# A fused cross-attention and ternary feed-forward kernel: loads issued earlier, and value products of two key chunks issued in pairs

## What is computed

```python
q = rope((layernorm(x) @ Wq)); k, v = split(ctx @ Wkv); k = rope(k)
w = softmax(q k^T / 4)
x = x + (w v) @ Wout + bout
u = layernorm(x)
h = gelu(bitlinear(u, w_fc))
out = x + bitlinear(h, w_proj)
# bitlinear(x, w): layer norm, x_hat = clip(x*128/max|x|) * max|x|/128,
#                  w_hat = sign(round(w/(mean|w|+eps))) * mean|w|
```

## Time and profile before

| | before |
|---|---|
| median of 3 runs | 849.15 us |
| the profiled execution | 848.58 us, span 846.5 us |
| projection, first scores | 0 to about 142 us |
| first turned scores | 172.8 us |
| last weighing of values | 556 us |
| rows | to 846.5 us |
| PE busy | 784.4 us (93%) |
| DVE busy | 681.3 us (80%) |
| ACT busy | 454.3 us (54%) |
| POOL busy | 337.8 us (40%) |

### The profile page before, as it was taken

The page is one execution under the profiler, slowest core; times in us unless marked ns, Lnnn a source line. Parts: engine busy times, 40 slices in busy tenths (PEclk is TensorE's granted clock), DMA queues, the critical chain, the costliest instruction groups (busy, mean ns, idle before and its releaser), DMA issues.

```text
span 846.5 us, 11693 instructions
## 1 busy us (share of the span) xinstructions
PE 784.4 (93%) x3842; PEld 334.0 (39%) x3842; DVE 681.3 (80%) x937; ACT 454.3 (54%) x825; POOL 337.8 (40%) x428
## 2 busy tenths in 40 slices
PE   1999997499999999999999989887999999999995
PEld 0788885023223223222232222233444444444442
DVE  5888885588888888888888868157999899988883
ACT  4466664067777777777777757642322432233230
POOL 3688875364445544555444535312222111111000
PEclk9999998589999999999999989999999999999999
DMA  8288877634455555676655773224466535654463
GB/s 273 83 216 233 253 189 168 163 90 118 120 154 149 143 155 135 148 144 163 163 143 142 201 134 85 71 74 79 110 117 137 120 87 108 112 117 88 83 128 88
DMA packets 175579, 116.14 MB, mean 137 GB/s; under 512 B 116512, under 2 KB 147232, under 8 KB 175520
## 3 DMA queue, kind: packets, MB, share of 16 engines
q1 hardware_dynamic: 175520, 115.40, 56.1%
HBM read 64.50 MB, written 25.43 MB: 106 GB/s over the span
## 4 chain that ended last, share of the span: by engine, by line
PE 80%; DVE 7%; DMA 5%; SPq 3%; ACT 2%; issue 2%; POOL 1%; DVEq 0%; POOLq 0%; ACTq 0%
PE banks L638 15%; PE banks L625 14%; PE banks L599 12%; PE banks L879 11%; PE banks L867 10%; PE banks L256 9%; PE banks L853 5%; DMA stack_words<-max_rows 2%; PE banks L280 1%; SPq L230 1%; DVE h_scales L945 1%; SPq L526 1%; ACT probs_words L689 1%; PE banks L246 1%; DVE probs_words L954 1%
## 5 line engine op out<-in xcount | busy, mean ns | idle before, releaser
L669 DVE TENSOR_REDUCE maxima<-banks 128x2 f32<-128x1024 f32 x256 | 302.1, 1216 | 67.2 <-PE banks L599 67.1
L689 ACT ACTIVATE probs_words<-banks 128x512 f32<-128x512 f32 x512 | 276.3, 597 | 105.3 <-PE banks L625 103.5
L625 PE MATMUL banks<-stack_words 98*128 98x512 bf16 x512 | 175.7, 386 | 6.6 <-DMA stack_words<-max_rows 4.6
L599 PE MATMUL banks<-stack_words 96*128 96x512 bf16 x512 | 160.8, 397 | 9.1 <-DMA stack_words<-k_parts 4.8
L638 PE MATMUL banks<-probs_words,late_words 128*32 128x512 f32 x1024 | 137.2, 608 | 0.5
L867 PE MATMUL banks<-ternary_words,late_words 128*128 128x512 f16 x512 | 114.6, 382 | 8.1 <-DMA late_words<-late_words 8.1
L879 PE MATMUL banks<-ternary_words,stack_words 128*128 128x512 f16 x512 | 114.6, 383 | 5.4 <-DMA stack_words<-stack_words 5.4
L995 ACT ACTIVATE probs_words<-probs_words,h_moments 128x2048 f32<-128x2048 f32 x16 | 32.0, 2002 | 130.9 <-DVE h_moments L937 130.9
L625 PEld LDWEIGHTS banks<-stack_words 98*128 98x128 bf16 x512 | 39.4, 97 | 147.9 <-ACT probs_words L689 85.4
L599 PEld LDWEIGHTS banks<-stack_words 96*128 96x128 bf16 x512 | 50.0, 100 | 73.9 <-DVE maxima L669 12.3
L879 PEld LDWEIGHTS banks<-ternary_words,stack_words 128*128 128x128 f16 x512 | 50.3, 99 | 71.4 <-issue 15.3
(11 more groups left out here) (123 smaller groups left out, 935.0 us busy)
## 6 DMA issues: line engine op xcount, KB each, us to landing
o_rows<-late_words SPq DMA_DIRECT2D x32, 256.0 KB, 2.7
k_parts<-ternary_words SPq DMA_DIRECT2D x48, 128.0 KB, 2.5
q_parts<-ternary_words SPq DMA_DIRECT2D x48, 128.0 KB, 2.4
stack_words<-q_parts SPq DMA_DIRECT2D x32, 192.0 KB, 2.9
stack_words<-k_parts SPq DMA_DIRECT2D x96, 64.0 KB, 2.7
stack_words<-k_parts SPq DMA_DIRECT2D x32, 192.0 KB, 2.8
attn_words<-in_x_dram SPq DMA_DIRECT2D x16, 256.0 KB, 4.1
probs_words<-in_L_ffn_w_fc_dram SPq DMA_DIRECT2D x16, 256.0 KB, 3.6
```

The lines of the kernel that those rows point to most:

```text
L599: mm = self.nc.tensor.matmul(self.score_slot[j % 2][:, i], self.mem.q_stack[0:STACK, slot, head, c * P:(c + 1) * P], self.mem.k_stack[0:ST ...
L625: self.nc.tensor.matmul(self.mem.banks[:, self.ST_BANK[k]], self.mem.k_stack[0:STACK + 2, slot, head, c * P:(c + 1) * P], self.mem.q_stack ...
L669: dve.tensor_reduce(self.maxima[:, g % 2, 2 * j:2 * j + 2], self.score_slot[j % 2], AX.X, ALU.max).then_inc(self.scores_read, 1)
L689: act.activation(self.probs[:, c, head, :], self.mem.banks[:, self.ST_BANK[k]], ACT.Exp, scale=1 / math.sqrt(HEAD)).then_inc(self.exp_done, 1)
```

## The change

In `tensor_step` the four chunks of values are no longer weighed one at a time at c = 0, 1, 2, 3 but two at once at c = 0 and two at c = 2. On SP the weights of the first two blocks and two of the first four stacks are loaded before the projection's end, the loads of Wout, its bias and the first rows of x are spread over eight steps. On POOL the first `split_maxima` stands ahead of the first `ternarise`, and two divisions later. On DVE `save_sums` follows the second reduction of a step instead of the first, and the last inversion stands one step later. On ACT the first `centre_u` stands among the exponentials.

```diff
--- before.py
+++ after.py
@@ -649,9 +649,11 @@
             if 0 <= turned < GROUPS:
                 self.scores_turned(pe, turned, 4 * c + 1)
             if c == 0 and before >= 0:
-                self.weigh_v(pe, before, CHUNKS - 1)
-            if c > 0 and 0 <= turned < GROUPS:
-                self.weigh_v(pe, turned, c - 1)
+                self.weigh_v(pe, before, 2)
+                self.weigh_v(pe, before, 3)
+            if c == 2 and 0 <= turned < GROUPS:
+                self.weigh_v(pe, turned, 0)
+                self.weigh_v(pe, turned, 1)
             if 0 <= turned < GROUPS:
                 self.scores_turned(pe, turned, 4 * c + 2)
                 self.scores_turned(pe, turned, 4 * c + 3)
@@ -808,11 +810,14 @@
 
 
 
-    def load_weights(self, sp, wout, bout):
+    def load_bias(self, sp, bout):
         sp.wait_ge(self.att.v_staged, 3 * HG)
-        sp.dma_start(self.wout_sb, wout.rearrange("(k p) n -> p k n", p=P)).then_inc(self.wout_loaded, DMA)
         sp.dma_start(self.bout_sb, bout.rearrange("(a d) -> a d", a=1).to_broadcast([P, DIM])
                      ).then_inc(self.bout_loaded, DMA)
+
+    def load_weight(self, sp, wout, k):
+        sp.wait_ge(self.att.v_staged, 3 * HG)
+        sp.dma_start(self.wout_sb[:, k], wout[k * P:(k + 1) * P]).then_inc(self.wout_loaded, DMA)
 
     def load_x(self, sp, x, n):
         need(sp, self.x1_ready, n - 1)
@@ -845,7 +850,7 @@
         att = self.att
         pe.wait_ge(att.divided, (n // CHUNKS + 1) * KX)
         if n == 0:
-            pe.wait_ge(self.wout_loaded, DMA)
+            pe.wait_ge(self.wout_loaded, KX * DMA)
             pe.wait_ge(att.scores_read, GROUPS * 2 * GH)
         need(pe, self.x1_ready, n - 1)
         c = n % CHUNKS
@@ -1044,13 +1049,19 @@
                     prj.load_x(sp, x, s)
                 if within(s - 2, TILES):
                     prj.load_piece(sp, w_fc, w_proj, s - 2)
+                if s == TILES + 4:
+                    sp.wait_ge(prj.projected[1], TILES)
+                    att.load_weight(sp, w_fc, w_proj, 0)
+                    att.load_weight(sp, w_fc, w_proj, 1)
                 if within(s - 5, TILES) and (s - 5) % 2 == 1:
                     prj.store_parts(sp, s - 5)
-                if s >= TILES + 6 - STACK_SLOTS:
-                    att.load_stacks(sp, s - TILES - 6 + STACK_SLOTS)
+                if s in (14, 16):
+                    att.load_stacks(sp, s // 2 - 7)
+            att.load_stacks(sp, 2)
+            att.load_stacks(sp, 3)
 
             for s in range(GROUPS + 3):
-                if s < GROUPS:
+                if 2 <= s < GROUPS:
                     att.load_weight(sp, w_fc, w_proj, s)
                 if STACK_SLOTS <= s < GROUPS:
                     att.load_stacks(sp, s)
@@ -1058,10 +1069,12 @@
                 if within(s - 2, GROUPS):
                     att.load_max(sp, s - 2)
                     att.turn_weight(sp, s - 2)
-                if s == GROUPS - 4:
-                    rows.load_weights(sp, wout, bout)
-                    rows.load_x(sp, x, 0)
-                    rows.load_x(sp, x, 1)
+                if s == GROUPS - 7:
+                    rows.load_bias(sp, bout)
+                if GROUPS - 6 <= s < GROUPS - 2:
+                    rows.load_weight(sp, wout, s - GROUPS + 6)
+                if GROUPS - 2 <= s < GROUPS:
+                    rows.load_x(sp, x, s - GROUPS + 2)
             rows.load_x(sp, x, 2)
             rows.turn_u(sp, 0)
 
@@ -1160,7 +1173,7 @@
 
             for s in range(1, GROUPS):
                 for j in range(2 * GH):
-                    if j == 1 and s >= 3:
+                    if j == 2 and s >= 3:
                         att.save_sums(dve, s - 3)
                     if j == 4 and s >= 7 and s % 2 == 1:
                         att.invert_sums(dve, (s - 7) // 2)
@@ -1188,7 +1201,7 @@
                     rows.second_h(dve, s - 1)
                 if s < TILES:
                     rows.statistics(dve, s)
-                if s == 1:
+                if s == 2:
                     att.invert_sums(dve, PAIRS - 1)
 
         @block.scalar
@@ -1227,8 +1240,8 @@
                         att.exponentials(act, s - 2, k)
                     if k == att.HALFWAY - 1 and within(s - 1, GROUPS):
                         att.save_max(act, s - 1)
-                if s == GROUPS + 1:
-                    rows.centre_u(act, 0)
+                    if k == 3 and s == GROUPS + 1:
+                        rows.centre_u(act, 0)
             rows.centre_u(act, 1)
 
             for s in range(TILES + 1):
@@ -1274,8 +1287,11 @@
             for s in range(GROUPS + 1):
                 if s >= 1:
                     att.stage_v(pool, s - 1)
+                if s == 0:
+                    att.split_maxima(pool, s)
                 if s < GROUPS:
                     att.ternarise(pool, s)
+                if 1 <= s < GROUPS:
                     att.split_maxima(pool, s)
                 if s >= 10 and s % 2 == 0:
                     att.divide(pool, (s - 10) // 2)
@@ -1284,9 +1300,8 @@
             rows.add_bias(pool, 1)
             att.divide(pool, 12)
             rows.spread_u(pool, 0)
+            rows.add_bias(pool, 2)
             rows.spread_u(pool, 1)
-            att.divide(pool, 13)
-            rows.add_bias(pool, 2)
 
             for s in range(TILES + 1):
                 if within(s - 1, TILES):
@@ -1295,8 +1310,8 @@
                     rows.spread_u(pool, s + 1)
                 if 3 <= s + 3 < TILES:
                     rows.add_bias(pool, s + 3)
-                if s in (3, 5):
-                    att.divide(pool, PAIRS - 2 + (s - 3) // 2)
+                if s in (1, 3, 5):
+                    att.divide(pool, PAIRS - 3 + s // 2)
 
 
 # ---- launch: one core; inputs and outputs as the reference has them ----
```

## The result

The changed kernel takes **870.11 us** (median of 4 runs, 869.26 to 870.84) against 849.39 us for the kernel before (4 runs, 848.03 to 849.91): a ratio of **1.0246**, with a 95% interval of 1.0228 to 1.0264. It is slower, by 20.7 us; 868 us was forecast. The profiled execution took 870.84 us with a span of 868.7 us, 22.2 us more than the span before.

A forecast was written before the change was run, and what follows sets the result against it. PE was taken as first by a narrow margin over DVE, with DVE setting the paired step. Terms 33.0 + 4.7 - 11.0 - 1.0 - 3.2 - 3.5 = +19.0 gave 868 us, range 855 to 882, chance 0.70.

The forecast's parts named there:

- Direction and cause: Whole kernel: slower, chance 0.86, since paired products leave DVE a 3.72 us hole with 2.26 us of work, twice a step.
- The rival that PE alone sets the step: Attention steps: PE's own 11.23 us is the step, 812 us in total; chance 0.09.
- The rule of the Trainium skill named in the prediction: PE: a change of the tiling mode drains TensorE; pairing takes away half of such drains.
- The copy: DVE's copy of the sums, 0.64 us, behind the second reduction delays reductions 2 and 3, for which PE waits.
- The second rival: Attention steps: the copy hides after all, step 12.4 us, total +1.7 or 851 us; chance 0.06.
- The step: Steady attention: 13.0 us a step, 29 steps 377.0 us against 343.95, +33.0 us.
- the stall of the earlier trace: Step that loads Wout: PE's 3.81 us wait for a small DMA, expected to vanish, contained in the +33.0.
- Start: Start of attention: first scores up to 4.8 us earlier, first turned scores at 161.1 instead of 172.84, -11.0 us taken.
- Step 2: Attention step 2: one product less ahead of its transpose, -1.0 us.
- Last steps: Steps 32 to 34, paced by ACT: pairs cost +4.7 us; the earlier `centre_u` spares 3.2 before the first `expand`.
- A clock that falls: Steady steps: PE standing still 1.8 us a step loses its clock, 886 us or above; chance 0.08.
- Passage: Passage into rows: -3.5 us beside `centre_u`'s -3.2; third `expand` waits 2.9 instead of 4.91 and keeps its clock, 1.5.

The follow-up runs named there:

- pairs alone: Kernel before with only the value products issued two at once in `tensor_step`, copy of the sums still behind the first reduction: 868.46 us, ratio 1.0234.
- half the maxima: Changed kernel with each reduction of maxima on DVE reading only 256 of 512 keys: 843.75 us in one run, steps of 11.99 us.
- half the exponentials: Changed kernel with ACT's exponentials over only 256 of 512 queries: 862.16 us in one run, steps of 12.87 us.
- both others halved: Changed kernel with maxima over half of the keys and exponentials over half of the queries: 825.28 us in one run, steps of 11.56 us.
- the copy where it was: Changed kernel with the copy of the sums back ahead of reduction 1, products still in pairs: 851.65 us, ratio 1.0028, steps of 12.27 us.
- the copy late: Kernel before with only the copy of the sums moved behind reduction 1, products single: 884.05 us in one run, steps of 12.82 us.
- close score pairs: Changed kernel with the copy of the sums first and score pairs issued close before and behind each pair of products: 835.94 us, ratio 0.9836.
- single products and moved loads: Changed kernel with products and copy put back as before: 830.16 us, ratio 0.979; again 829.3 us; with division 13 one tile earlier, 829.36 us.

## Why the prediction was right, and where it was not

**Direction and cause.** Both hold. DVE idles 1.48 and 1.44 us in each step, 1.46 was worked out; a pair takes 1.85 us (401.10 to 402.95) instead of 1.89; with the way in, 0.32 us (400.78 to 401.10), a change of kind costs what it cost before. The pair alone loses 19 us (pairs alone), and only less work on DVE, not on ACT, shortens the step (half the maxima, half the exponentials). The rival that PE alone sets the step falls: no step came to 11.23, not even with both others halved. The rule of the Trainium skill named in the prediction (TensorEngine Tiling (Array Packing), Key Properties) agrees with the trace as far as it goes: each change spared saves a way in of some 0.1 us. What the order does to other engines it does not say.

**The copy.** That it belongs to the loss because it delays a reduction for which PE waits holds: 0.6 us a step, 12.87 against 12.27. Only reduction 2 is in the loop (the score pair at 400.34 waits for it); reduction 3, which the prediction named too, is not. The second rival, a copy that hides, was the right time for another kernel: in its old place the copy does hide, and that kernel's 851.65 us is the 851 given there.

**The step, 13.0 foreseen, 12.87 measured.** The prediction's sum gave 13.1, or 12.95 with reductions closer together. The term that was mis-sized most is the reciprocal, 0.13 us a step, which I counted with DVE's work; the reductions and the copy were 0.05 and 0.04 less than 9.40 and 0.64. The reciprocal stands ahead of a reduction that is not in the loop. The next step of DVE's timeline in the changed kernel has it:

```profile
414.20 0.34 DVE L677 RECIPROCAL sums<-sums 128x32 f32<-128x32 f32 x1
...
416.90 4.74 DVE L671 TENSOR_REDUCE maxima<-banks 128x2 f32<-128x1024 f32 x4 [1.27 <-PE banks L599]
```

DVE idles 1.27 us instead of 1.48, and the reductions begin at 416.90, 12.87 us after those at 404.03, as without it. The first of the 29 steps took 12.06 us, the others 12.87. So 29 steps cost +28.5, not +33.0, with the stall of the earlier trace rows gone as foreseen. Not foreseen was how near ACT is: in one half of the step it holds up the turned scores too, and with half the maxima it sets the step, 0.9 us below DVE's limit.

**Start.** −11.1 for −11.0. The shift of the first scores was smaller, 138.76 us against 141.92, so 3.2 of the 4.8 us: DVE waited 2.46 us for a tile of x in the projection. The path behind it was shorter than worked out. Step 2 was to gain 1.0 and lost 0.5: its first 6.1 us ran at the lower clock, where before it was 2.8 us.

**Last steps.** The first `expand` came 4.3 us later where 1.5 was forecast. Of these, 1.3 and 1.6 us are the two slow pairs. That they count in full is borne out by the kernel with the copy where it was, which has one slow pair, 1.2 us longer than the others: from its last transpose (534.59) to the first `expand` (562.12) it takes 27.53 us, the changed kernel 29.31 (552.81 to 582.12), so 1.78 more for 1.75 us more of slow time. Without the slow pairs the 4.3 are 1.3: the sum of the terms for ACT's pace and for `centre_u`, 1.5, was nearly right. A clock that falls stood in the prediction as a rival for the steady steps, where it never fell; it fell where PE waits for ACT again and again.

**Passage.** This term failed. The addition for tile 2 no longer waits for POOL, but the wait ahead of the third `expand` only fell from 4.91 to 4.00, not to 2.9, since the division I had called covered now ran beside DVE's scaling and lengthened it by 0.97 us. The next division did the same to the scaling at 631.78 us (2.25 us), with no wait of PE behind it. And the clock, which I had expected to stay up after 2.9 us, fell after 4.00 and even after 3.14 us (8.77 both times), though not after 3.15 in the earlier trace rows, 7.08. In the kernel before with the copy late, the first `expand`, at the same place as that of the earlier trace rows, waited 3.12 us and took 8.77. So −3.5 became about 0.1. Against the forecast the terms are off by −4.5 (the steps), +1.4 (start and step 2), +2.8 (last steps) and +3.6 (passage and rows): the sum is +3.3. That 868 lies so near 870 is in part luck: errors of both signs met.

**What stays open.** Whether an order of PE exists in which the pair gains: one other was tried. Why the clock falls after one wait of 3.1 us and not after another is open, and so is why two pairs of products in the last steps meet the lower clock.

## What to carry to other kernels

Ask of a regrouping that makes the busiest engine cheaper how long its consumers are left without input, and compare that with the work that their filled buffers hold: two slots of 1.175 us against a hole of 3.7 us gave the step to within 1%. Write the loop out through both engines; only what stands in it counts, so that a copy of 0.6 us moved by one place cost 18 us and a reciprocal beside it nothing. A change with several independent parts should be timed part by part: here one was worth −19 us and was hidden under the rest.

## What the runs showed of the hardware

- The granted clock fell without any long pause of PE. Ahead of the slow pair at 554.23 PE's waits for ACT were 0.26, 0.19 and 0.18 us, ahead of the one at 570.46 they were 0.26, 0.71 and 0.58. Such a slow pair, of 2.7 to 3.6 us, stands in the last steps of five kernels with pairs (twice in the changed kernel and with close score pairs, once with pairs alone, with the copy first and with half the maxima), and in no kernel with single products and moved loads. Another slow pair of the kernel with pairs alone, at 507.90, followed a wait of 2.90 us for a DMA and is of another kind: in the kernel before, a single product behind the stall of the earlier trace rows was slow too, 1.94 us instead of 1.06. In both kernels with half the exponentials, one run each, no pair is slow though all stand in pairs. So pairs alone don't bring it about; that pairs and ACT's full work together do is a guess.
- A scaling on DVE (128x2048 f32, 1.29 us) that started 0.1 us after a division on POOL (1.27 us) took 2.26 us, and 1.29 when the division was moved away. The Trainium skill (SBUF — State Buffer, SBUF: two separate sides) has the two engines share a pair of ports by an exclusive lock: a DVE instruction in a 2-port perf mode and a GpSimd instruction block each other fully, whichever starts later waiting. No run here shows which mode the scaling runs in. If it is such a one, it would have waited 1.17 us and worked 1.29, 2.46 in all, an estimate by that page's rule; the trace has 0.2 less, and so agrees nearly. In the kernel with half the exponentials the delay goes both ways: a scaling that started 0.03 us after an addition on POOL took 2.32 us, and the division behind that addition 2.25 us instead of 1.27.
